# Sandwich of attention and a six-layer FFN stack: three stages in written-out form, their work spread over the engines

## The reference

```python
x = x + _layernorm(attention(_layernorm(x)))     # x: 4 x 1024 x 128 f32
x = x + _layernorm(ffn_stack(_layernorm(x)))
```

## Time and profile before

| | us |
|---|---|
| median of 3 runs | 4380.38 (4378.44 to 4381.74) |
| profiled execution, its own time | 4380.54 |
| its span, first to last instruction | 4378.7 |
| TensorE busy | 4132.4 (94%) |
| VectorE busy | 3601.4 (82%) |
| ScalarE busy | 3593.7 (82%) |
| GpSimd busy | 2336.7 (53%) |

### The profile page before, as it was taken

How to read it: one execution, slowest core, us unless ns; L and a number is a source line. 1 busy time by engine, 2 the same in 40 slices (tenths; PEclk the granted TensorE clock), 3 DMA queues, 4 the chain that set the end, 5 groups by cost and what they waited for, 6 DMA issues and landing times. The chain is left out here.

```text
span 4378.7 us, 124836 instructions
## 1 busy us (share of the span) xinstructions
PE 4132.4 (94%) x44000; PEld 2958.4 (68%) x44000; DVE 3601.4 (82%) x8420; ACT 3593.7 (82%) x6842; POOL 2336.7 (53%) x2840
## 2 busy tenths in 40 slices
PE   4799999975999999999999999999999999999993
PEld 2466666653777777777777777777777777777773
DVE  6588888876888888888888888888888888888884
ACT  1799989952888888888888888888888888888882
POOL 1000000005776767676677676767776777667761
PEclk7899999986999999999999999999999999999996
DMA  6777777731111111111111111111111111111111
GB/s 226 220 224 236 230 223 237 224 116 65 46 41 46 36 43 41 46 41 46 33 46 41 46 41 41 38 46 41 46 36 43 41 46 41 42 37 46 41 46 45
DMA packets 258632, 358.17 MB, mean 82 GB/s; under 512 B 44404, under 2 KB 216156, under 8 KB 257884
## 3 DMA queue, kind: packets, MB, share of 16 engines
q1 hardware_dynamic: 258140, 351.55, 26.7%
HBM read 151.19 MB, written 93.34 MB: 56 GB/s over the span
## 5 line engine op out<-in xcount | busy, mean ns | idle before, releaser
L1375 PE MATMUL la_ps<-la_Wqkv,la_xsT 128*128 128x512 f32 x2304 | 1191.1, 612 | 2.9 <-DVE la_rsk L1089 1.6
L1032 POOL TENSOR_TENSOR la_rt<-la_rt,la_rn 128x1024 f32<-128x1024 f32 x384 | 722.9, 1904 | 27.5
L1089 DVE TENSOR_TENSOR la_rsq<-la_ps,la_tab 128x1024 f32<-128x1024 f32 x384 | 469.2, 1222 | 93.5 <-ACT la_sq L1233 91.3
L1096 DVE TENSOR_REDUCE la_ssum<-la_sq 128x8 f32<-128x512 f32 x768 | 502.4, 674 | 0.0
L1410 PEld LDWEIGHTS la_ps<-la_kT,la_qB 128*64 128x64 f32 x12288 | 390.5, 138 | 145.8 <-issue 145.8
L1233 ACT ACTIVATE la_sq<-la_ps 128x512 f32<-128x512 f32 x768 | 448.8, 597 | 43.6 <-PE la_ps L1375 30.2
L1375 PEld LDWEIGHTS la_ps<-la_Wqkv,la_xsT 128*128 128x128 f32 x2304 | 377.4, 190 | 141.3 <-issue 94.0
L1089 DVE TENSOR_TENSOR la_rsk<-la_ps,la_tab 128x1024 f32<-128x1024 f32 x384 | 466.1, 1214 | 6.1 <-ACT la_sq L1233 3.9
L1441 PEld LDWEIGHTS la_ps<-la_Wo,la_oT 128*128 128x128 f32 x3072 | 366.7, 192 | 110.2 <-issue 103.4
L481 POOL COPY at_vh<-V 128x64 f32 (+1 forms) x64 | 15.2, 238 | 786.2 <-PE at_ps L680 785.4
L1410 PE MATMUL la_ps<-la_kT,la_qB 128*64 128x64 f32 x12288 | 433.2, 224 | 0.0
(11 more groups left out here) (168 smaller groups left out, 10204.4 us busy)
## 6 DMA issues: line engine op xcount, KB each, us to landing
at_band<-skew_scratch SPq DMA_DIRECT2D x64, 1536.0 KB, 7.3
la_vs<-la_v SPq DMA_DIRECT2D x192, 384.0 KB, 3.6
skew_scratch<-at_R SPq DMA_DIRECT2D x64, 1024.0 KB, 6.7
la_vs<-la_v SPq DMA_DIRECT2D x192, 128.0 KB, 3.4
la_Wqkv<-in_wqkv SPq DMA_DIRECT2D x28, 384.0 KB, 3.7
kt_scratch<-pr_k SPq DMA_DIRECT2D x24, 384.0 KB, 3.2
qt_scratch<-pr_q SPq DMA_DIRECT2D x24, 384.0 KB, 4.1
at_qh<-qt_scratch SPq DMA_DIRECT2D x64, 144.0 KB
```

Source lines behind the costliest of these rows:

```text
L1032: e.tensor_tensor(heads(rt, w), heads(rt, w), wide(rn[:, w * H:(w + 1) * H], D), ALU.mult)\
L1089: e.tensor_tensor(dst.rearrange("p f (h d) -> p f h d", d=D), ps[:, c % 2, :].rearrange("p (h d) -> p h d", d=D).unsqueeze(1).to_broadcast ...
L1096: e.tensor_reduce(ssum[:, c * 8:(c + 1) * 8], sq[:, c % 2, :].rearrange("p (h d) -> p h d", d=D), AX.X, ALU.add).then_inc(ss_ev.sem, 1)
L1375: e.matmul(ps[:, c % 2, :], xsT[:, m * P:(m + 1) * P], Wqkv[:, ds(layer(n) % 2, 1), c * 512:(c + 1) * 512], start=True, stop=True)\
```

## The change

The three small stages lose their loops: every step is written out, every buffer has two copies (index `u`, step modulo 2), and each engine has its own order of steps with lags. `norms` makes a pair of Norms that share their signals but not their statistics. In the projections ScalarE applies the norm, evacuates q and k twice each (to f32 and to the first bf16 part), GpSimd splits q, VectorE splits k. The scratch tensors hold the parts of k three times instead of nine and those of q five times; each head's rows are picked by the load's access pattern. The output stage moves inside `layers`: SP issues the layers' loads ahead of its stores, GpSimd clears the layers' tiles between its roots, `vs` lends room, the bias is a matmul of one row, and GpSimd adds X. `rsq` and `rsk` now lie in X2. The last stage loads X2 in eight parts; ScalarE applies, GpSimd adds.

```diff
-    def __init__(self, part, name, n):
+    def __init__(self, part, name, n, first=None):
...
+        if first:
+            self.power, self.cell, self.set, self.chain = first.power, first.cell, first.set, first.chain
+            self.stats, self.rstd = first.stats, first.rstd
+            return
...
-    qt_d = nc.dram_tensor("qt_scratch", [PARTS, PARTS, P, B * S], BF16).ap()
-    kt_d = nc.dram_tensor("kt_scratch", [PARTS, PARTS, P, B * S], BF16).ap()
+    qt_d = nc.dram_tensor("qt_scratch", [H_A, 2 * PARTS - 1, D_A, B * S], BF16).ap()
+    kt_d = nc.dram_tensor("kt_scratch", [H_A, PARTS, D_A, B * S], BF16).ap()
...
 def first_projections(nc, a, X, V, ident, qt_d, kt_d, rel_d, skew):
...
         @block.sync
...
+            x_loaded(0)
+            for dst, src in ((ident, "c_ident"), (Wq, "L0_attn_Wq"), (Wk, "L0_attn_Wk"), (Wv, "L0_attn_Wv")):
...
+            for b in range(1, B):
+                x_loaded(b)
...
+            for n in range(STEPS):
+                u, to = n % 2, ds(n * G * P, G * P)
+                e.wait_ge(k3_ev.sem, k3_ev.v(n))
+                for p in range(PARTS):
+                    e.dma_start(kt_d[:, p, :, to], k3[:, u, p, :]).then_inc(k_out[u].sem, 16)
+                e.wait_ge(q3_ev.sem, q3_ev.v(n))
+                for p in range(2 * PARTS - 1):
+                    e.dma_start(qt_d[:, p, :, to], q3[:, u, p % PARTS, :]).then_inc(q_out[u].sem, 16)
...
         @block.gpsimd
...
+                for n, u in steps(i, 3):
+
+                    e.wait_ge(q_ev.sem, q_ev.v(n))
+                    e.tensor_tensor(qf[:, u, :], qf[:, u, :], q3[:, u, 0, :], ALU.subtract).then_inc(c_q.sem, 1)
+                    e.wait_ge(c_q.sem, c_q.v(n, 1))
+                    e.tensor_tensor(q3[:, u, 1, :], qf[:, u, :], unit[:].to_broadcast([P, G * P]), ALU.mult)\
+                        .then_inc(c_q.sem, 1)
+                for n, u in steps(i, 0):
+                    ln[u].root(e, n)
+                for n, u in steps(i, 3):
+                    e.wait_ge(c_q.sem, c_q.v(n, 2))
+                    e.tensor_tensor(q3[:, u, 2, :], qf[:, u, :], q3[:, u, 1, :], ALU.subtract).then_inc(q3_ev.sem, 1)
...
         @block.scalar
...
+                    for g in range(G):
+                        act = e.activation(xh[:, u, g, :], tile(n, g), ACT.Identity, bias=mr[:, u, g, :],
+                                           scale=ln[u].st[:, g, 8:9])
...
+                    if n >= 2:
+                        e.wait_ge(q3_ev.sem, q3_ev.v(n - 2))
+                        e.wait_ge(q_out[u].sem, q_out[u].v(n // 2 - 1))
+                    e.activation(qf[:, u, :], ps[:, BANK_Q + u, :], ACT.Identity, bias=bqs[:, 0:1], scale=-SC_A)
+                    e.activation(q3[:, u, 0, :], ps[:, BANK_Q + u, :], ACT.Identity, bias=bqs[:, 0:1], scale=-SC_A)\
+                        .then_inc(q_ev.sem, 1)
...
-def first_output(nc, a, X, X2, ident, x2_d):
+def first_output(nc, a, X, X2, ident, x2_d, ps, room, loads, zeros, casts):
...
+            @block.gpsimd
...
+                zeros(e, 0)
+                for i in range(STEPS + 2):
+                    for n, u in steps(i, 0):
+                        ln1[u].root(e, n)
+                    for n, u in steps(i, 1):
+                        e.wait_ge(yn_ev.sem, yn_ev.v(n))
+                        x = X[:, slot(n * G):slot(n * G) + G, :].rearrange("p g d -> p (g d)")
+                        e.tensor_tensor(x2(n), x, yn[:, u, :], ALU.add).then_inc(x2_ev.sem, 1)
+                    for n, u in steps(i, 2):
+                        ln2[u].root(e, n)
+                    for n, u in steps(i, 0):
+                        zeros(e, n + 1)
...
+                        e.matmul(ps[:, BANK_Y + u, :], one[:], bo4[:], start=True, stop=False)
...
-        rsq, rsk, rt = t.sb("rsq", [P, 2, INNER]), t.sb("rsk", [P, 2, INNER]), t.sb("rt", [P, 2 * INNER])
+        rsq, rsk = (X2[:, w * NT // 2:(w + 1) * NT // 2, :].rearrange("p (u a) d -> p u (a d)", u=2) for w in range(2))
+        rt = t.sb("rt", [P, 2 * INNER])
...
+        first_output(nc, a, X, X2, ident, x2_d, ps, vs, loads, zeros, casts)
+        block = t.block()
...
-def last_output(nc, X, x2_d, out):
+def last_output(nc, X, X2, x2_d, out):
...
+        @block.gpsimd
...
+                for n, u in steps(i, 0):
+                    ln[u].root(e, n)
+                for n, u in steps(i, 2):
+                    e.wait_ge(yn_ev.sem, yn_ev.v(n))
+                    e.wait_ge(x2_in[n], 16)
...
+                    e.tensor_tensor(res[:, u, :, :], X2[:, n * G:(n + 1) * G, :], yn[:, u, :, :], ALU.add)\
                         .then_inc(res_ev.sem, 1)
...
+            for i in range(STEPS):
+                e.dma_start(X2[:, i * G:(i + 1) * G, :], x2_d[:, i * G:(i + 1) * G, :]).then_inc(x2_in[i], 16)
```

More of the change, by code:

```diff
@@ L184, in build @@
         ident = top.enter_context(nc.sbuf_tensor("ident", [P, P], F32))
[L185 to L191, removed]
+        X2 = top.enter_context(nc.sbuf_tensor("X2", [P, NT, E], F32))
+        with nc.sbuf_tensor("V", [P, NT, E], F32) as V:
+            first_projections(nc, a, X, V, ident, qt_d, kt_d, rel_d, skew)
+            first_attention(nc, a, V, X2, ident, qt_d, kt_d, rel_d, skew)
+        layers(nc, a, X, X2, ident, x2_d)
+        last_output(nc, X, X2, x2_d, out)
 def first_projections(nc, a, X, V, ident, qt_d, kt_d, rel_d, skew):
@@ L445, in heads_in @@
                 hd = n % HEADS_A
-                row, col = ds(hd % H_A * D_A, D_A), ds(hd // H_A * S, S)
-                for dst, src in ((qh, qt_d), (kh, kt_d)):
-                    e.dma_start(dst[:, m, :], src.rearrange("a b p c -> (a b) p c")[:, row, col])\
+                col = hd // H_A * S
+                for dst, src, step in ((qh, qt_d, D_A * B * S), (kh, kt_d, 0)):
+                    head = src[ds(hd % H_A, 1), 0:PARTS, :, ds(col, S)].rearrange("h a d c -> (h a d) c")
+                    rows, line = list(head.ap)
+                    e.dma_start(dst[:, m, :], bass.AP(head.tensor, head.offset, [rows, [step, PARTS], line]))\
                         .then_inc(qk_in[m % 2].sem, 16)
@@ L853, in layers @@
+def layers(nc, a, X, X2, ident, x2_d):
     with Part(nc, "la") as t:
@@ L919, in two, with loads @@
             return x.rearrange("p (k d) -> p k d", k=2)
-        @block.sync
-        def _(e):
-            for mark in vs_in + ys_in:
-                mark.open(e)
+        def loads(e):
             for dst, src in ((lng, "lngT"), (lnb, "lnbT"), (b1, "b1T"), (mask32, "c_mask"), (rot, "c_rot")):
@@ new lines, in _ @@
+        @block.scalar
+        def _(e):
+            for n in range(STEPS):
+                u = n % 2
+                e.wait_ge(mr_ev.sem, mr_ev.v(n))
+                if n >= 2:
+                    e.wait_ge(res_ev.sem, res_ev.v(n - 2))
+                for g in range(G):
+                    act = e.activation(yn[:, u, g, :], X[:, slot(n * G + g), :], ACT.Identity,
+                                       bias=mr[:, u, g, :], scale=ln[u].st[:, g, 8:9])
+                act.then_inc(yn_ev.sem, 1)
@@ L1611, in _ @@
+            for n in range(STEPS):
+                u = n % 2
+                e.wait_ge(res_ev.sem, res_ev.v(n))
+                e.dma_start(rows[:, n * G:(n + 1) * G, :], res[:, u, :, :]).then_inc(sent[u].sem, 16)
             for mark in sent:
```

544 lines of the change are left out of this document (274 added, 270 removed).

## The result

The changed kernel takes 4307.7 us (median of 4 runs, 4305.0 to 4309.4) where the kernel before took 4379.8 beside it (4378.4 to 4381.7): a ratio of 0.983, 95% interval 0.982 to 0.984. That is 72 us less; the forecast was 4296 (84 less), its range 4280 to 4315. The profiled execution of after took 4309.4 with a span of 4307.6, against 4380.5 and 4378.7 before.

What follows compares the result with a forecast made beforehand. Attention and layers, TensorE-bound, hold 4140 of 4379 us, hardly touched; VectorE paces the first projections. Savings 32.5 + 1 + 28.2 + 21.3 = 83.0 from 4380.5 give 4297.5, called 4296 for slack in waits; range 4280 to 4315.

Steps and rivals of the forecast that it cites:

- A ring remains ... 11.1 / 2 = 5.6: First projections: q's evacuation, GpSimd's turn, five issues and landing precede the evacuation two steps on; 5.6 us a step.
- both of the bounds of the forecast, 5.6 and 6.8: First projections: a step takes at least 5.6 us (ring) and at most 6.8 (TensorE at low clock); 6.3 taken.
- VectorE's casts over 1 us: Sign that the forecast is wrong, pointing to rival 1; a 128x512 cast took 0.42 us with GpSimd idle.
- GpSimd's 128x512 operations over 1.6 us: Sign that the forecast is wrong; it took 1.28 us for each of q's operations in the first projections.
- ScalarE's idle before q's evacuation put down to the q writes: First projections: sign that the forecast is wrong, meaning a ring longer than 5.6 us.
- Rival 1: Three small stages: GpSimd and VectorE operations exclude each other, 14.4 us more, 4310 us; chance 0.24.
- 5.1, with waits 5.3: Output stage: GpSimd's two roots, addition and share of memsets take 5.1 us a step, 5.3 with waits.
- stays 3287 us within 5: Layers: sign that the forecast is right, their stretch unchanged at 3287 us within 5.
- Rival 3: Layers: rsq and rsk in X2's place slow the tiles; kernel slower from 0.43 us more a tile; chance 0.02.
- Now GpSimd has root and addition, 2.3 ... I take 2.4: Last stage: GpSimd's 2.3 us, above ScalarE's 1.95 and VectorE's 1.7, gives a 2.4 us step; 21.3 us won.
- rival 2: Small stages: rings of two buffers set the pace, steps 8.0, 8.0 and 3.2 us, 4338 us in all; chance 0.08.
- the forecast's own bracket: Whole kernel: 4280 to 4304 us around the forecast of 4296, chance 0.62; 4304 to 4315 was rival 1's.

Runs made afterwards that it cites:

- The third copy: Changed kernel with three copies instead of two of q's and k's f32 tile and parts in the first projections: 4302.9 us, stage end 67.37.
- the kernel of all gains: Changed kernel with three q/k copies, q's writes first, three sets of norm signals in the last stage, rsq and rsk in own memory: 4292.2 us, ratio 0.980.
- the two edits above: Changed kernel, output stage: bias product ahead of TensorE's wait (4310.6 us, stage 56.9), or GpSimd's addition in two halves (4308.8, stage 56.6); one execution each.
- the last-stage order's kernel: Changed kernel with the mean's product of step n-1 ahead of step n's statistics on VectorE in the last stage: 4309.4 us, one execution.
- the version with halves: Changed kernel with GpSimd's output-stage addition of 128x512 as two of 128x256: 4308.8 us, one execution.
- the bias-first kernel: Changed kernel with TensorE's bias product ahead of the wait for ScalarE's copy in the output stage: 4310.6 us, one execution.

## Why the prediction was right, and where it was not

**First projections, 32.5 forecast, 28.4 measured.** The failed step is "A ring remains ... 11.1 / 2 = 5.6". Evacuation and GpSimd's turn were 1.4 + 4.9 there and 6.30 in the trace. Left out were SP's wait for k's part and k's three writes ahead of q's, 2.5 us; mis-sized were the issues, 0.49 taken from the fills and 0.61 to 0.64 measured (+0.7), and the landing, 2.3 against 1.9. The sum is 13.9, not 11.1: a step of 6.95 that lies above both of the bounds of the forecast, 5.6 and 6.8. Seven steps cost 48.4 instead of 44.1, and the tail (k's writes again) 13.3 instead of 10.5. The start gave 3.1 back: the first evacuation came at 14.07, not 17.2, since the table load ran ahead of the wait, the first product came at 8.21 instead of 9.8, and four applications in a row took 1.65 instead of 4 x 0.484. Of the signs, "VectorE's casts over 1 us" did not come (at most 0.66), "GpSimd's 128x512 operations over 1.6 us" came once in 24 (1.68; their mean is 1.24 against the 1.28 forecast), and "ScalarE's idle before q's evacuation put down to the q writes" came six times.

**Rival 1** was right in the thing, and in the changed kernel mostly wrong in the place. The groups of VectorE in the stage, against the earlier trace rows:

```profile
L340 DVE TENSOR_TENSOR pr_k<-pr_kf,pr_k 128x512 bf16<-128x512 f32 x8 | 8.0, 997 | 0.1
...
L330 DVE CAST pr_k<-pr_kf 128x512 bf16<-128x512 f32 x8 | 4.5, 568 | 0.0
L334 DVE SCALAR_TENSOR_TENSOR pr_mr<-pr_lnb_stats 128x4 f32<-128x4 f32 x4 | 3.4, 844 | 3.0 <-POOL pr_lnb_stats L135 2.9
```

k's last subtraction, 0.68 by itself, takes 1.0 in the mean (k's first stays at 0.69), a cast of 0.42 takes 0.57, a product of 0.16 takes 0.84. But most of that lay beside the ring. In the turn shown above the waits of GpSimd make 0.6 of the 13.9 us (line 290 takes 1.47 there instead of 1.04, the root 1.19 instead of 1.01), and in three of the eight steps k's last subtraction, for which SP waits ahead of q's writes, takes 1.5. The third copy took 8.5 us out of the stage with both engines as busy as before (VectorE 43.5 us for 42.5, GpSimd 42.0 for 41.0). Where the ring no longer binds, in the kernel of all gains, GpSimd sets the step, and the ports are 1.0 of its 5.36 us.

**Attention**: 1.7 won, 1 forecast; over the twelve profiles of the changed kernel and its versions it ranges from 849.2 to 853.4, so that neither is told from chance.

**Output stage and opening**: forecast 57.7 us after attention's end, measured 57.7, and the term on which it rests ("5.1, with waits 5.3", GpSimd's) is what the two edits above confirm. Part of the match is luck. TensorE's granted clock in the second 8 us of the stage was 0.50 here and 0.88 in another execution (the last-stage order's kernel), its products with Wo 2.08 and 1.16 us:

```profile
938.76 2.08 PE L866 MATMUL la_ps<-ou_Wo,la_vs 128*128 128x128 f32 x8
```

```profile
935.32 1.16 PE L866 MATMUL la_ps<-ou_Wo,la_vs 128*128 128x128 f32 x8
```

The stage took 54.9 to 55.0 us in the four profiles with 0.88 to 0.93 there, and 57.7 in the four with 0.50; its code was the same in all eight.

**Layers**: "stays 3287 us within 5" holds with 3290.7. Rival 3 may be right in kind, for rows now show durations that go with the placement of tiles, but in size it is at most 3.5 / 192 = 0.02 us a tile, where it needed 0.43.

**Last stage, 21.3 forecast, 16.7 measured.** The failed step is "Now GpSimd has root and addition, 2.3 ... I take 2.4": it takes the busiest engine for the bound. The order on VectorE with two sets makes 3.27. GpSimd's order also puts the root of step 2, which waits for this loop, ahead of the first addition: that one ended 8.9 us after the layers, not 7.7, and the other seven took 20.1 us, not 16.8, since the last two no longer go round the loop. It is rival 2's mechanism with its 3.2, in this one stage; and SP's order is what made a ring of two copies the bound in the first. With both mended the kernel lands at 4292, near the 4296 forecast for the one without.

**The number.** 4307.7 lies within 4280 to 4315, but above the 4304 at which the forecast's own bracket ended, in the one set aside for rival 1, and it came there mainly by the two loops of two copies and not by rival 1's ports. That is luck, and so is that the first stage missed by only 4.1 us: its ring and tail cost 7.1 us more than forecast, and the earlier start gave 3.1 back.

## What to carry to other kernels

A ring is as long as everything its releasing queue does in between, so put into its sum all that is issued ahead of its own transfers, and issue the transfers of the tightest ring first. With two copies and engines in a fixed order, follow one turn of the loop through each engine's order before taking the busiest engine's work for the step. Keep short VectorE operations that others wait for out of the moment in which a long GpSimd instruction starts.

## What the hardware showed that I had not expected

VectorE's small operations don't slow down beside GpSimd, they wait for the end of the instruction that runs: 0.16 us become 1.22 beside an addition of 512 columns, 0.68 beside 256 (in the version with halves) and 0.42 beside 128. It goes the other way too: GpSimd's root takes 1.49 instead of 1.01 when it starts beside one of VectorE's subtractions, its own subtraction 1.67 instead of 1.15. The Trainium skill says so ("SBUF — State Buffer", Who interferes with whom): the pair of ports that both use is an exclusive lock, held for the whole instruction. These runs agree with it. The page also says that an operation with two SBUF inputs is caught only by a GpSimd instruction that reads SBUF. In the timeline of after the product (two inputs) runs through a memset unharmed, while in the bias-first kernel line 130, with one tensor input, is caught by one and ends with it (961.92 against 961.89):

```profile
938.57 1.80 POOL L1018 MEMSET la_v<- 128x2048 f32 x1
938.65 0.17 DVE L898 SCALAR_TENSOR_TENSOR ou_mr<-ou_ln_stats 128x4 f32<-128x4 f32 x1 [1.12 <-POOL ou_ln_stats L135]
```

```profile
960.09 1.80 POOL L1023 MEMSET la_qB<- 128x2048 f32 x1
...
961.04 0.88 DVE L130 TENSOR_SCALAR ou_ln1b_stats<-ou_ln1b_stats 128x4 f32<-128x4 f32 x1
```

An issue on SP costs 0.61 to 0.64 us for the writes of k and q (128 KB) and 0.49 for the fills of 192 KB; why was not tried. And GpSimd's additions of 512 columns take 1.2% longer in the change, with rsq and rsk in X2's memory, than before; which tile's place does it is open.
